# Eleven experts instead of twelve ahead of the first scan, and a chunk's front in three pairs

## The reference, cut to what matters

```python
h = _layernorm(x) * (1 + ca) + sa
x = x + ga * _L0_attn_ref(h, ...)     # decayed attention and a small FFN
h = _layernorm(x) * (1 + cb) + sb
x = x + gb * _L0_ffn_ref(h, ...)      # 8 experts of width 512, two weighted per token
h = _layernorm(x) * (1 + ca) + sa
x = x + ga * _L1_attn_ref(h, ...)     # Mamba: the part below
h = _layernorm(x) * (1 + cb) + sb
x = x + gb * _L1_ffn_ref(h, ...)      # one sparse spectral matrix and a bias
```

## Time and profile before

| | us |
|---|---|
| median of 3 runs | 566.05 |
| lowest and highest | 565.32, 568.63 |
| the profiled execution | 565.65 |
| its span | 563.5 |

### The profile page before, as it was taken

How to read it: one execution, slowest core, us unless ns; L and a number is a source line. 1 busy time by engine, 2 the same in 40 slices (tenths; PEclk the granted TensorE clock), 3 DMA queues, 4 the chain that set the end, 5 groups by cost and what they waited for, 6 DMA issues and landing times.

```text
span 563.5 us, 6814 instructions
## 1 busy us (share of the span) xinstructions
PE 466.0 (83%) x2324; PEld 327.2 (58%) x2324; DVE 430.1 (76%) x706; ACT 342.8 (61%) x461; POOL 348.1 (62%) x250
## 2 busy tenths in 40 slices
PE   4879898689899999988889988879979757397566
PEld 4457566345788887766766666756767532042224
DVE  5789998963542541169897799998799998989994
ACT  1445253433655564699998999988999738453310
POOL 3137997946404123316496669798668898789561
PEclk9998897999999999999999999999999959787998
DMA  8800000000000000402846853668554568731100
GB/s 274 332 1 0 1 1 2 0 0 0 1 1 2 0 2 1 151 1 73 189 112 135 204 149 83 145 140 177 152 151 112 135 149 172 199 81 69 56 0 19
DMA packets 15601, 48.93 MB, mean 87 GB/s; under 512 B 2320, under 2 KB 7824, under 8 KB 12624
## 3 DMA queue, kind: packets, MB, share of 16 engines
q0 software_dynamic: 3024, 22.02, 19.5%
q1 hardware_dynamic: 11968, 25.58, 13.3%
q10 hardware_dynamic: 576, 0.92, 0.5%
HBM read 25.31 MB, written 1.18 MB: 47 GB/s over the span
## 4 chain that ended last, share of the span: by engine, by line
PE 33%; DVE 30%; ACT 12%; POOL 10%; issue 9%; DMA 4%; POOLq 0%; SPq 0%; DVEq 0%; ACTq 0%
PE pO L1368 9%; DVE Hs L824 7%; DVE S L709 6%; DVE pCT L811 5%; POOL ZS L394 4%; PE pY L1423 4%; DVE pH L708 3%; DMA Acc<-ZS 3%; PE pH L1356 3%; ACT gel L1072 3%; ACT dA L1084 3%; ACT L1084 2%; PE pH L1358 2%; PE pH L1357 2%; POOL ln_x L359 2%
## 5 line engine op out<-in xcount | busy, mean ns | idle before, releaser
L1368 PEld LDWEIGHTS pO<-w_e,gel 128*128 128x128 f32 x1024 | 122.2, 192 | 13.9 <-issue 8.7
L1368 PE MATMUL pO<-w_e,gel 128*128 128x128 f32 x1024 | 124.7, 276 | 1.3 <-DVE X L795 1.0
L824 DVE TENSOR_TENSOR_SCAN Hs<-dA,HL,pCT 128x512 f32<-128x512 f32 x96 | 117.7, 1267 | 6.3 <-POOL ZS L394 3.2
L1072 ACT ACTIVATE gel<-pH,b_e 128x512 f32<-128x512 f32 x128 | 86.1, 687 | 40.1 <-PE pH L1358 39.3
L1084 ACT ACTIVATE dA<-dt,a_neg 128x512 f32<-128x512 f32 x128 | 81.9, 711 | 21.8 <-DVE Hs L824 21.5
L394 POOL TENSOR_TENSOR ZS<-Hs,Crow 128x1024 f32<-128x1024 f32 x31 | 74.9, 2428 | 30.3 <-DVE Hs L824 28.8
L811 DVE TENSOR_TENSOR pCT<-u,pB 128x1024 f32<-128x1024 f32 x64 | 78.3, 1224 | 10.0 <-PE pB L1448 8.9
L1356 PE MATMUL pH<-h2h,w_e1h 128*128 128x512 f32 x128 | 57.5, 449 | 21.4 <-ACT gel L1072 20.3
L795 DVE SCALAR_TENSOR_TENSOR X<-pO,wts,X 128x128 f32<-128x128 f32 x128 | 36.0, 344 | 44.2 <-PE pO L1368 43.5
L394 POOL TENSOR_TENSOR Zev<-Hs,Crow 128x1024 f32<-128x1024 f32 x26 | 62.7, 2426 | 8.3 <-DVE Hs L824 7.7
L1448 PE MATMUL pB<-ST,sel 96*128 96x512 bf16 x64 | 26.6, 415 | 38.8 <-DVE pCT L811 38.6
(11 more groups left out here) (251 smaller groups left out, 851.7 us busy)
## 6 DMA issues: line engine op xcount, KB each, us to landing
Crow<-c_rows SPq DMA_DIRECT2D x32, 512.0 KB, 4.2
Acc<-ZS POOLq DMA_DIRECT2D x12, 1024.0 KB, 8.8
Acc<-Zev POOLq DMA_DIRECT2D x9, 1024.0 KB, 7.4
w_e<-in_w_e SPq DMA_DIRECT2D x2, 2048.0 KB, 10.6
X<-in_x SPq DMA_DIRECT2D x4, 256.0 KB, 7.7
S<-in_w_mod ACTq DMA_DIRECT2D x2, 384.0 KB, 5.6
out<-h2T SPq DMA_DIRECT2D x3, 256.0 KB, 2.8
w_cx<-in_conv_row SPq DMA_DIRECT2D x1, 512.0 KB, 8.8
```

What stands on the lines that cost most here:

```text
L824: vec.tensor_tensor_scan(Hs[:, 2 * o + d, 0:w], dA[:, 4 * (p % 2) + 2 * o + d, 0:w], pU[:, d, 0:w], HL[:, d, n:n + 1] if c else 0.0, ALU.m ...
L1072: nc.scalar.activation(gel[:, n % NG, 0:w], pH[n % 2][:, 0:w], ACT.Gelu_apprx_tanh, bias=b_e1[:, NK * e + k:NK * e + k + 1]).then_inc(s["m ...
L1368: ins = mm(pO[:, j * P:(j + 1) * P], gel[:, n % NG, j * P:(j + 1) * P], w_e2[:, NK * (g % E) + k, :], start=(k == 0 and j == 0), stop=(k = ...
```

## The change

`AHEAD` becomes 11. So the pairs are 11 with an expert alone, 21 with both and 11 with two states alone. `ALONE`, the first pair without an expert, becomes 21 (before, 20), and `TOT` stays at 24.

The front of a chunk moves into pairs k = 5, 6 and 7: `ln_stats` from the middle of 4 to the middle of 5, `ln_turn` from "U" of 5 to the end ("C") of 5, `rows` from "B" of 5 to "U" of 6, both halves of the convolution into pair 6 ("A" and "B"; before, "A" of 5 and "A" of 6), `dt_part` to "U" and "A" of 7 (before, "B" and "C" of 6), and `step` from the middle to the end of 7. Counted in experts and not in pairs, `ln_stats` stays where it was for chunk 0, behind the addition of expert 7.

GpSimd's five instructions of the split are one function again, and it runs at the head of its pair, ahead of `output(2p)`. ScalarE runs `dt_part` between `hidden(2, 3)` and `decays(p+1)`.

```diff
-AHEAD = 12
+AHEAD = 11
...
-ALONE = (NL * E - AHEAD) // 2 * 2
+ALONE = NL * E - AHEAD
...
-                    plan += [(4, "mid", "ln_stats", front), (5, "U", "ln_turn", front, 1),
-                             (5, "A", "x_part", front, 0), (5, "B", "rows", front), (6, "mid", "rows_low", front), (6, "A", "x_part", front, 1),
-                             (6, "B", "dt_part", front, 0), (6, "C", "dt_part", front, 1), (7, "mid", "step", front)]
+                    plan += [(5, "mid", "ln_stats", front), (5, "C", "ln_turn", front, 1),
+                             (6, "U", "rows", front), (6, "A", "x_part", front, 0), (6, "B", "x_part", front, 1),
+                             (7, "U", "dt_part", front, 0), (7, "A", "dt_part", front, 1), (7, "end", "step", front)]
...
                 link(pool.tensor_tensor(P1[64:96, 0:w], bc[64:96, :], st[64:96, :], ALU.subtract))
-
-            def rows_low(c):
-
-                w = WIDTHS[c]
-                st, bc = ST[:, c % 2, 0:w], BCf[:, c % 2, 0:w]
-                for name, count in done.items():
-                    if count:
-                        pool.wait_ge(s[name], count)
                 link(pool.tensor_tensor(bc[64:96, :], bc[64:96, :], st[64:96, :], ALU.subtract))
...
             for p, stages in later_stages():
+                for _, stage, c, *_ in stages:
+                    if stage == "rows":
+                        rows(c)
                 if 0 <= p < NL * NP:
                     output(p, 0)
...
-            def run(p, stages, places):
+            def run(p, stages, places, steps=False):
 
                 for at, stage, c, *k in stages:
-                    if at not in places:
+                    if at not in places or (stage == "dt_part") != steps:
                         continue
...
                     hidden(p + AHEAD, (2, 3))
+                run(p, stages, "UA", True)
                 if 0 <= p + 1 < NL * NP:
                     decays(p + 1)
```

More of the change, by code:

```diff
@@ L538, in run @@
                         close()
-                    if (at in ("B", "C", "end")) == last and stage in ("ln_stats", "ln_last", "rows", "rows_low", "route", "gate", "bias"):
-                        {"ln_stats": ln, "ln_last": lambda c: ln(c, True), "rows": rows, "rows_low": rows_low, "route": route, "gate": gate, "bias": bias}[stage](c)
+                    if (at in ("B", "C", "end")) == last and stage in ("ln_stats", "ln_last", "route", "gate", "bias"):
+                        {"ln_stats": ln, "ln_last": lambda c: ln(c, True), "route": route, "gate": gate, "bias": bias}[stage](c)
             for p, stages in later_stages():
+                for _, stage, c, *_ in stages:
+                    if stage == "rows":
+                        rows(c)
                 if 0 <= p < NL * NP:
```

## The result

| | before | after |
|---|---|---|
| median, runs | 567.13 us, 4 | 574.71 us, 4 |
| lowest and highest | 565.32, 568.63 | 573.81, 577.01 |
| the profiled execution | 565.65 | 577.01 |
| its span, mean granted clock of TensorE | 563.5, 0.956 | 574.8, 0.943 |

The change makes the kernel slower: the ratio is 1.0147, with a 95% interval of 1.012 to 1.0175, some 8 us. I had forecast 567.9 with a range up to 572.5. The profiled execution of after is the slowest of its four (the spans of the others are 571.7 to 572.6), so the two profiles differ by 11.3 us where the medians differ by 7.6.

The account below looks back on a forecast made before the run. The bound was taken to change by stretch: TensorE ahead of the first scan and at chunk fronts, VectorE elsewhere. Terms -5.0 + 1.4 + 1.9 + 3.5 = +1.8 gave 567.9 us on the median, range 561.5 to 572.5.

Parts of the forecast that it names:

- Part 1: Start, one expert fewer ahead: first product at 240.4 instead of 245.41, -5.0 us (bounds -4.2 and -5.6).
- Part 2: Front of chunk 1, pairs 4 to 7: 44.35 us against 42.95, +1.4 (bounds 0 and +3).
- a sign that I had named: Prediction is wrong if GpSimd's split starts more than 0.8 us later than 5.7 into pair 6.
- Part 3: Chunk 2, pairs 12 to 15: 46.7 us against 44.77, +1.9 (bounds 0 and +3).
- the same walk: Chunk 1's step-by-step timing reused for chunk 2 with scans of 2.45 instead of 2.33: 36.3 us from pair 13's start.
- Part 4: Chunk 3, pairs 20 to 23: 43.4 us against 39.92, +3.5 (bounds +1 and +7).
- the second sign that I had named: Prediction is wrong if the clock of pairs 21 and 22 differs from before.
- A: Rival: fronts cost what they did, new waits replacing old, only the 1.2 us addition extra: 562.3 us; chance 0.24.
- B: Rival: TensorE stays at 1.2 GHz through both halves in pair 22, some 7 us later: 575 us; chance 0.13.
- C: Rival: rows or decays of chunk 0 hold the first scan at its old time, only costs remain: 572.5; chance 0.06.
- D: Rival: ScalarE's table switch costs a second 1.28 us at four boundaries, 5.1 more: 573.0 us; chance 0.02.
- GpSimd's split as hidden in chunks 1 and 2: The scans' 4 us wait behind split and output lies inside the expert wait, costing nothing, 0.8 us to spare.

Follow-up runs that it names:

- experiment 1: The changed kernel's new front, but with twelve experts ahead as before: 582.32 us, ratio to before 1.0301.
- experiment 4: The changed kernel with the accumulation DMA of pair k = 4 started one pair later, behind GpSimd's normalisation: 576.81 us, ratio to before 1.0192.
- experiment 10: The kernel of experiment 8 without any idle matmuls: 565.87 us, ratio to before 1.001.
- experiment 5: The kernel of experiment 2 with its three idle matmuls of pair 0 also in pairs 8 and 16: 569.91 us, ratio to before 1.0074.
- experiment 3: The changed kernel with GpSimd's split behind the first output of its pair instead of ahead: 574.78 us, ratio to before 1.0157.
- experiment 8: The changed kernel with transposes half a pair later, rows ahead of the convolution, halves apart, split behind first output, and idle matmuls: 565.05 us, ratio to before 1.0.
- experiment 6: The kernel of experiment 5 with GpSimd's split behind the first output: 570.71 us, ratio to before 1.0084.
- experiment 2: The changed kernel with two or three idle matmuls ahead of a front's transposes and three in pair 0: 570.75 us, ratio to before 1.0093.

## Why the prediction was wrong, point by point

- **Part 1, -5.0: right.** The first product came at 239.89 instead of 240.4, -5.5, inside the bounds. `ln_turn`'s wait came as forecast (1.38, forecast 1.5); softplus ended at 238.5 and not 239.2, part of it because expert 8 ended 0.3 earlier than in the profile of before (215.26 against 215.53). Profiles of the same code differ by 1.6 us at this mark, so the agreement to 0.5 is in part luck.
- **Pairs 0 to 3, taken as unchanged: +1.35 in the profiled execution.** The new place of the softplus, ahead of four decays, makes the gelu of expert 11 late: TensorE waits 2.90 us, and runs the rest of pair 0 at the 1.2 GHz level. It isn't a fixed cost: the same wait kept the clock in the profiles of experiments 1, 4 and 10.
- **Part 2, +1.4 (0 to +3): +2.8.** The waits of 5.07 for GpSimd, 1.06 for the expert and 1.68 for the softplus (forecast 4, about 1 and 1.9) are the ones named. The split started 7.3 into pair 6 (302.67 against 295.34), not 5.7: this is a sign that I had named as making the prediction wrong. The normalisation had ended 11.45 after pair 5's start and not 10.75, behind a wait of 1.20 for an accumulation.
- **Part 3, "the same walk", +1.9 (0 to +3): +6.1. This is the step that failed.** I carried the end of the normalisation (10.75 after the pair's start) and the full clock from chunk 1 into chunk 2. There GpSimd had a wait of 3.28 for the accumulation's transfer ahead of it, and the normalisation ended at 12.75; TensorE, which used to have two blocks up to do in that time, waited 3.35 and fell to the 1.2 GHz level; the expert was added at 30.8 from the pair's start, where the walk had 26.6. Pair 16 started 39.6 after pair 13 and not 36.3, and pair 12 took 11.3 and not 10.4. Of the 4.2 us that the forecast missed, 2.6 to 2.9 went with the clock: experiments 1 and 5, whose transposes of chunk 2 kept it, take 48.3 and 48.0 there.
- **Part 4, +3.5 (+1 to +7): +7.6**, a miss of 4.1 and as large as that of part 3. The wait of the transposes (3.59, forecast 3.3), the wait for the split (3.19, forecast 3) and `step` (3.40, forecast 3.34) are right in size, though experiment 3 shows that the split's wait covered one for a B row and cost only 0.7. The convolution was mis-sized: I took half clock for part of the first half only and its end at 25.0; both took 9.40 and ended at 27.2, and the second product of pair 23 waited 2.70 and started at 29.5, not 26.2. The granted clock of pairs 21 and 22 was 0.78 and 0.50, against 0.50 and 0.89 before: the second sign that I had named.
- **The sum.** Forecast +1.8 on the profiled execution, measured +11.3 there and 7.6 between the medians. The errors of parts 2 to 4 have one sign, and I read this so: each piece of the new front hangs on the one ahead of it, and a late normalisation delays transposes, rows, split, convolution and step together. The bounds added reached 575; I cut the range at 572.5 as if the three parts would miss independently.
- **The rivals.** A (562.3) is refuted for this order; with another one (experiment 8) the fronts cost 4.4 in place of A's 1.2. B (575) named the right resource, and pair 22 did run at 0.50, but that its time fits is luck: the halves took 9.40 and not 2 x 6.9, only 4.1 of its 7 us came in chunk 3 (+7.6 against the +3.5 forecast), and another 4.2 came in chunk 2, where it expected none. C is refuted by the first product. D is refuted: softplus starts 0.02 us after its load's end in after too (load at 235.97 for 1.28, activation at 237.27). The Trainium skill, page "ScalarE: Activation LUTs", section "What ACT_TABLE_LOAD costs", adds a drain of 1.38 us to each switch; no row of this case shows one.
- **GpSimd's split as hidden in chunks 1 and 2: shown** by experiments 3 and 6.
- **How much is clock and how much order.** The idle matmuls take the ratio from 1.0147 to 1.0074 (experiment 5), the new order of experiment 10 takes it to 1.001 with no idle matmul at all. These two overlap; they are not two terms of a sum. Why the other three runs of after are some 2 to 3 us shorter than the profiled one (spans of 571.7 to 572.6) is open: they have no trace. Their mean granted clock (0.936 to 0.943) is no higher than its 0.943, which speaks against a kept clock as the reason.

## What to carry to other kernels

A walk through one chunk's order is not a walk through the next: before a moved step is costed, look for each chunk at what stands ahead of it on the engine that feeds it, here a DMA wait in GpSimd's queue. When a waiting instruction is moved to the end of an engine's pair, the work that covered its wait is gone, and on TensorE the wait can be paid twice, once as time and once in clock (the wait of 3.35 us in chunk 2; that of 2.03 in chunk 1 kept the clock). The longest wait of a profile may only cover another: experiment 3 took away 5 us of it and gained nothing, while the new order of experiment 10 gained 1.3%. And eleven experts ahead, worth some 4 us at the start, are eaten up by what is left of the fronts' cost: no order tried here came out ahead of the kernel before.

## What the runs showed of the hardware

- The same wait of 2.90 us of TensorE in pair 0 was followed by matmuls of 0.63 (the 1.2 GHz level) in the profiles of after and of experiment 3, and of 0.39 in those of experiments 1, 4 and 10. The clock after this wait can't be read off the wait: a single profile shows it as 0 or as 1.35 us. Likewise in pair 8: a wait of 2.55 us kept the clock in after (next matmul 0.50), one of 2.53 us lost it in experiment 2 (0.79).
- `step` (128x1024, two SBUF inputs) took 1.23 alone, 1.64 and 1.74 or 2.84 where it met part of a GpSimd output, 3.40 behind one, and 4.39 beside two that ran back to back. The Trainium skill, page "SBUF — State Buffer", section "SBUF: two separate sides", says that a VectorE operation with two SBUF inputs and a GpSimd operation that reads SBUF exclude each other for a whole instruction. The times agree: each of the five is, within 0.02 us, 0.15 less than the rest of GpSimd's output at `step`'s start plus the 1.23 of `step` alone. In the last, 4.39 - 1.23 = 3.16 us is more than the 2.35 of one output, so two of GpSimd's outputs went first.
